# Cross attention and a 4-bit dense layer on one core: the softmax weights are turned by VectorE in squares of 32 and regrouped through DRAM, instead of by TensorE transposes

## What is computed

```
q = layernorm(x) @ Wq        # 32 heads of 128
k = ctx @ Wk; v = ctx @ Wv   # 8 heads of 128, each shared by 4 query heads
q, k = rope(q, pos), rope(k, pos)
scores = q k^T / sqrt(128), set to -1e9 where mask == 0
attn = softmax(scores);  x = x + concat(attn v) @ Wo
x = x + layernorm(x) @ dequantize(qweight, qzeros, scales) + bias
```

## Time and profile before

| | |
|---|---|
| median of 3 runs | 2412.4 us (2410.72 to 2417.8) |
| the profiled execution's own time | 2418.64 us |
| its span, first to last instruction | 2416.8 us, granted clock 0.991 |
| PE busy | 2353.0 us, 97% |
| DVE, ACT, POOL busy | 1336.1, 1114.9, 1180.8 us (55%, 46%, 49%) |
| stage B (first `score` to last `out_copy`) | about 405 to 1596 us |
| mean DMA rate | 143 GB/s |

### The profile page before, as it was taken

How to read it: one execution, slowest core, us unless ns; L and a number is a source line. 1 busy time by engine, 2 the same in 40 slices (tenths; PEclk the granted TensorE clock), 3 DMA queues, 4 the chain that set the end, 5 groups by cost and what they waited for, 6 DMA issues and landing times.

```text
span 2416.8 us, 33647 instructions
## 1 busy us (share of the span) xinstructions
PE 2353.0 (97%) x11552; PEld 1975.2 (82%) x11552; DVE 1336.1 (55%) x1949; ACT 1114.9 (46%) x2515; POOL 1180.8 (49%) x926
## 2 busy tenths in 40 slices
PE   8999998999999999899999999989999999999999
PEld 6887877888888888688888888868887877878887
DVE  4762554666666666666666666637743233343532
ACT  3222123667676667666766667643332222322010
POOL 1410535555665665556665566555664344355110
PEclk9999999999999999999999999999999999999999
DMA  7676674333434335343343333368554454443111
GB/s 262 237 178 223 233 246 152 92 102 100 113 103 114 105 106 155 113 127 102 93 117 106 106 112 103 111 212 284 202 191 168 149 178 166 143 177 113 44 44 53
DMA packets 201241, 346.65 MB, mean 143 GB/s; under 512 B 17744, under 2 KB 126544, under 8 KB 201168
## 3 DMA queue, kind: packets, MB, share of 16 engines
q1 hardware_dynamic: 187088, 310.06, 41.0%
q10 hardware_dynamic: 13312, 33.56, 4.2%
q0 software_dynamic: 768, 2.10, 0.3%
HBM read 238.69 MB, written 106.97 MB: 143 GB/s over the span
## 4 chain that ended last, share of the span: by engine, by line
PE 81%; DVE 7%; DMA 5%; ACT 3%; POOL 3%; issue 1%; SPq 1%; ACTq 0%; DVEq 0%; POOLq 0%
PE ps L208 18%; PE ps L209 18%; PE ps L210 18%; PE ps L690 7%; PE ps L691 7%; PE ps L692 7%; PE ps L622 4%; DMA scores<-in_ctx 2%; DVE rows L1226 1%; DMA xc_scratch<-xring 1%; DMA wraw<-in_L_xattn_Wo 1%; DMA xring<-in_x_tiles 1%; POOL s_buf L1322 1%; ACT probs L864 1%; PE ps L714 1%
## 5 line engine op out<-in xcount | busy, mean ns | idle before, releaser
L208 PE MATMUL ps<-act_t,wq_t 128*128 128x512 f32 x1280 | 512.5, 400 | 20.8 <-DVE act_t L1076 10.9
L210 PE MATMUL ps<-act_t,wq_t 128*128 128x512 f32 x1280 | 501.8, 392 | 0.0
L209 PE MATMUL ps<-act_t,wq_t 128*128 128x512 f32 x1280 | 501.6, 392 | 0.0
L690 PE MATMUL ps<-b_parts,a_parts 128*128 128x512 f32 x896 | 353.1, 394 | 11.3 <-POOL b_parts L1395 5.1
L1322 POOL TENSOR_TENSOR rope_tmp<-rope_tmp 128x512 f32<-128x512 f32 x144 | 192.4, 1336 | 341.8 <-DVE rope_tmp L1013 341.7
L691 PE MATMUL ps<-b_parts,a_parts 128*128 128x512 f32 x896 | 350.1, 391 | 0.0
L692 PE MATMUL ps<-b_parts,a_parts 128*128 128x512 f32 x896 | 349.7, 390 | 0.0
L1171 DVE TENSOR_TENSOR a_parts<-xring,a_parts 128x1024 fp32r<-128x1024 f32 x112 | 147.8, 1320 | 349.7 <-ACT a_parts L889 349.7
L1395 POOL TENSOR_TENSOR b_parts<-wraw,b_parts 128x512 fp32r<-128x512 f32 x112 | 195.7, 1748 | 275.1 <-ACT b_parts L894 275.1
L889 ACT ACTIVATE a_parts<-xring 128x1024 fp32r<-128x1024 f32 x112 | 118.7, 1060 | 415.8 <-PE ps L692 407.8
L208 PEld LDWEIGHTS ps<-act_t,wq_t 128*128 128x128 f32 x1280 | 242.5, 189 | 69.7 <-DVE act_t L1076 11.4
(11 more groups left out here) (111 smaller groups left out, 4437.8 us busy)
## 6 DMA issues: line engine op xcount, KB each, us to landing
xring<-left_scratch SPq DMA_DIRECT2D x112, 512.0 KB, 3.5
left_scratch<-s_buf SPq DMA_DIRECT2D x64, 640.0 KB, 5.3
wraw<-in_L_xattn_Wq SPq DMA_DIRECT2D x64, 512.0 KB, 4.0
wraw<-in_L_xattn_Wo SPq DMA_DIRECT2D x64, 512.0 KB, 4.4
v_scratch<-kv_t ACTq DMA_DIRECT2D x32, 512.0 KB, 3.0
k_scratch<-kv_t ACTq DMA_DIRECT2D x32, 512.0 KB, 5.1
kv_t<-k_scratch SPq DMA_DIRECT2D x64, 256.0 KB, 5.1
kv_t<-v_scratch SPq DMA_DIRECT2D x64, 256.0 KB, 4.6
```

The lines of the kernel that those rows point to most:

```text
L208: eng.matmul(dst, lh, rh, start=(k == first), stop=False)
L209: eng.matmul(dst, lh, rl, start=False, stop=False)
L210: mm = eng.matmul(dst, ll, rh, start=False, stop=(k == last))
L690: pe.matmul(dst, lh, rh, start=(begins and not onto), stop=False, skip_group_check=True)
```

## The change

The eight `turn` transposes of a unit leave PE, except in the last four units (`tail`). In their place:

- DVE `transpose_squares` turns the weights in squares of 32x32 (one instruction of 128x1024) into `squares`; SP `store_squares` writes them to DRAM (512 KB), and when that has landed, SP `load_turned` reads them back with four DMAs, each of which fills 32 partitions (128 KB, in runs of 1 KB), which puts every square on its partitions; ACT `turned_hi` and POOL `turned_lo` (128x1024 each) make the two parts.
- `weigh` comes two units after its unit instead of one. The banks of scores and outputs are doubled, which the two banks of the transposes make room for.
- `masked` is now one instruction for each 128x256 that adds a mask (0 or -1e30) and takes the minimum of the negated sum (`tensor_tensor_reduce`, followed by a read of the accumulator); `exponents` uses scale -1.
- `out_copy` moves from ACT to DVE, `head_lo` from POOL to DVE (`next_head_lo`, behind `inverse_sum`). POOL's `combine` is spread over two units.
- The splitting of the second half's activations moves from group 7 to group 0: for each of eight pieces SP `load_centred`, ACT `split_piece`, DVE `rest_of_piece`, and two ACT-issued stores `store_parts`. Group 7 then loads high and low parts straight into `act_t` (sixteen DMAs of 512 KB, eight before unit 2 and eight before unit 4).

The core of the diff:

```
-            def weigh(G, u8, first=False):
+            def weigh(G, u8, fresh=False, tail=False):
...
-                    pe.wait_ge(o_copied, G * UPG + u8)
+                    pe.wait_ge(o_copied, G * UPG + (u8 - 1))
...
+                    pe.wait_ge(pt_lo, G * UPG + (u8 + 1))
...
+            def transpose_squares(G, u8):
+                par = u8 % 2
+                dve.wait_ge(p_ready, G * UPG + (u8 + 1))
+                dve.transpose(squares[par].rearrange("p (b k n i) -> p k n b i", b=4, k=2, n=4),
+                              probs[:, par, :, :, :].rearrange("p j q (k b i) -> p k (j q) b i", k=2, b=4)
+                              ).then_inc(squared, 1)
...
+            def store_squares(G, u8):
+                sp.wait_ge(squared, G * UPG + (u8 + 1))
+                sp.dma_start(sq_dram[u8 % 4], squares[u8 % 2].rearrange("p (b n) -> p b n", b=4)
+                             ).then_inc(sq_stored[u8 % 2], 16)
+
+            def load_turned(G, u8, first=False):
+
+                sp.wait_ge(sq_stored[u8 % 2], G * 64 + (u8 // 2 * 16 + 16))
+                if not first:
+                    hold(sp)
+                    sp.wait_ge(pt_lo, G * UPG + (u8 - 1))
+                for b in range(4):
+                    sp.dma_start(pt_raw[32 * b:32 * b + 32, u8 % 2, :].rearrange("i (a n) -> i a n", a=4),
+                                 sq_dram[u8 % 4, :, b, :].rearrange("(a i) n -> i a n", a=4)).then_inc(pt_in[u8 % 2], 16)
...
+            def turned_hi(G, u8, first=False):
+                act.wait_ge(pt_in[u8 % 2], G * 256 + (u8 // 2 * 64 + 64))
+                if not first:
+                    act.wait_ge(av_done, G * UPG + (u8 - 1))
+                act.activation(probs_t[u8 % 2][:, 0, :, :, :].rearrange("p a k n -> p (a k n)"), pt_raw[:, u8 % 2, :],
+                               ACT.Copy).then_inc(pt_hi, 1)
...
+            def turned_lo(G, u8):
+                pool.wait_ge(pt_hi, G * UPG + (u8 + 1))
+                hi, lo = [probs_t[u8 % 2][:, l, :, :, :].rearrange("p a k n -> p (a k n)") for l in range(2)]
+                pool.tensor_tensor(lo, pt_raw[:, u8 % 2, :], hi.bitcast(F32), ALU.subtract).then_inc(pt_lo, 1)
...
+            def load_centred(i):
+
+                if i > 0:
+                    sp.wait_ge(parts_stored, i * 32)
+                sp.dma_start(x_pair[0], xc_dram[i]).then_inc(xc_in, 16)
...
+            def split_piece(i):
+                act.wait_ge(xc_in, (i + 1) * 16)
+                act.activation(x_pair[1].bitcast(F32R), x_pair[0], ACT.Copy).then_inc(piece_hi, 1)
+
+            def store_parts(i):
+                act.wait_ge(piece_lo, i + 1)
+                act.dma_start(xp_dram[i, 0], x_pair[1]).then_inc(parts_stored, 16)
+                act.dma_start(xp_dram[i, 1], x_pair[0]).then_inc(parts_stored, 16)
...
+            def rest_of_piece(i):
+                dve.wait_ge(piece_hi, i + 1)
+                dve.tensor_tensor(x_pair[0].bitcast(F32R), x_pair[0], x_pair[1], ALU.subtract).then_inc(piece_lo, 1)
```

More of the change, by code:

```diff
@@ L406, in attention @@
                     p = (G - half * 8) * 2 + par
+                    tail = last and par == 1
                     if switch and u8 in (2, 4):
@@ L437, in attention @@
                             sp.dma_start(rope[:, c, :, :], rope_dram[1, c]).then_inc(rope_in[c], 16)
-                if not last:
-                    sp.wait_ge(av_done, G * UPG + UPG)
-                    load_v(g, HB - 1, nh)
-                else:
+                    if first and u8 > 0:
+                        load_centred(u8)
+                if last:
                     load_step(2)
                     load_step(3)
-                store_group(G * 4 + 3, half, (G - half * 8) * 2 + 1, 1, 1)
+                    for q in (62, 63):
+                        store_outputs(q, 31, q % 2)
+                        store_sums(q, 31, q % 2)
             def load_step(s):
@@ L628, in attention @@
                     i, pair = u8 % 4, G * 2 + (u8 // 4 + 1)
-                    more = not (last and u8 >= 4)
                     if u8 < UPG - 1:
-                        score(G, u8 + 1)
+                        score(G, u8 + 1, fresh=first and u8 == 0)
                     elif not last:
                         score(G + 1, 0)
-                    if u8 > 0:
-                        weigh(G, u8 - 1, first=first and u8 == 1)
+                    if last and u8 >= 4:
+                        if u8 < 6:
+                            weigh(G, u8 - 2)
+                        if u8 > 4:
+                            weigh(G, u8 - 1, tail=True)
+                        turn(u8)
+                        continue
@@ L636, in attention @@
+                    if switch and u8 in (4, 6):
+                        for k in range(2):
+                            pe.wait_ge(xp_in[2 * (u8 - 4) + k], 32)
+                    query(pair, i, 0, G * UPG + (u8 + 4))
+                    if u8 >= 2:
+                        weigh(G, u8 - 2, fresh=first and u8 < 4)
                     elif not first:
-                        weigh(G - 1, UPG - 1)
+                        weigh(G - 1, UPG + u8 - 2)
                     if switch and u8 in (4, 6):
-                        pe.wait_ge(x_lo, TT + 2 * (u8 - 4) + 2)
@@ L641, in attention @@
-                    if more:
-                        query(pair, i, 0, G * UPG + (u8 + 4))
-                    turn(G, u8, first=first and u8 == 0)
-                    if switch and u8 in (4, 6):
-                        pe.wait_ge(x_lo, TT + 2 * (u8 - 4) + 4)
-                    if more:
-                        query(pair, i, 1, G * UPG + (u8 + 4))
+                        for k in range(2, 4):
+                            pe.wait_ge(xp_in[2 * (u8 - 4) + k], 32)
+                    query(pair, i, 1, G * UPG + (u8 + 4))
@@ L661, in _ @@
             pe.wait_ge(kv_lo, UNITS_A)
[L662 removed]
+            score(0, 0, first=True, fresh=True)
             attention(0, first=True)
@@ L934, in attention @@
                         scaled(nG, nxt)
-            for m in range(3):
-                query_hi(0, 0, m, m)
+                    if first:
+                        split_piece(u8)
+            act.wait_ge(ident_in, 16)
+            act.activation(row_sum[:, 0, 0, 0:1], identity[:, 0:1], ACT.Exp)
+            query_hi(FIRST_TILES[0], 0)
+            head_hi(0, 10 * 16, (q_done, 2))
+            query_hi(FIRST_TILES[1], 1)
+            query_hi(FIRST_TILES[2], 2)
             exponents(0, 0)
-            head_hi(0, 10 * 16, (q_done, 3))
             scaled(0, 0)
@@ L1448, in _ @@
             attention(15, last=True)
-            combine(63, 1, (left_stored[0], 32 * 48))
+            for q in (62, 63):
+                for part in range(2):
+                    combine(q, q % 2, part)
             right_summed(2)
```

415 lines of the change are left out of this document (239 added, 176 removed).

## The result

| | before | after |
|---|---|---|
| median | 2413.01 us (2410.72 to 2417.8, 4 runs) | 2440.34 us (2434.39 to 2441.88, 4 runs) |
| profiled execution | 2418.64 us | 2434.39 us |
| its span, granted clock | 2416.8 us, 0.991 | 2432.6 us, 0.981 |

The ratio of the medians is 1.0105 (95% interval 1.0092 to 1.0117). The forecast was 2363 us, so its direction was wrong. The time lies inside the range for 8 in 10 (2325 to 2450), near its upper end, and outside the forecast's own 2340 to 2395. Both profiled executions lie some 6 us from their medians, on opposite sides: the traces show 15.8 us of loss where the medians show 27.3.

A forecast was written before the change was run, and what follows sets the result against it. PE, busy 97% of the span, was taken as the bound. From 2418.6 us, -108 + 17 + 45 - 7 + 0 + 4 = -49 gave 2369.6; the median, 6.2 lower, 2363 us, own range 2340 to 2395, 8 in 10 from 2325 to 2450.

The forecast's parts named there:

- What leaves PE: Attention units: 124 of 128 lose eight transposes, 0.87 us each, together 108 us; a unit falls from 9.14 to 8.27.
- The other engines' sums: Per attention unit: POOL 6.9 us, ACT 5.9, DVE 6.8 (bounds 6.1 to 8.4), to fit into 8.27.
- Hidden, then, with a thin margin: DRAM round trip of 7.7 us lands at T'+3.0, harmless until T'+3.1; T' is the next unit's score start.
- The first rival: Loops: the DRAM round trip becomes the bound, setting the pace from a trip of 9.0 us; slower; 2 in 10.
- ACT waiting for `pt_raw`: In the profile after: this wait in every unit would show that the round trip had become the bound.
- A wait of 0.5 us, once in four units: Loops: PE's `query` waits for `next_head_lo` on DVE, itself held by POOL's `turned_lo`; 17 us in all.
- Group 0: Piece loop of 14.7 us replaces 8.27 for seven rounds, +45 us; PE's 7.3 us idle start lies inside, -7.
- Group 7 at 0: Squares late by 7 to 9 us, 3 to 4 of it slack, twice; equals the old loss: 0, bounds -8 and +16.
- The queue's own sum: Loops: bytes per two units rise from 1920 to 3968 KB, DMA share from 38% to about 87%, an upper estimate.
- The end: After the attention: POOL has two whole `combine` ahead of the sums for step 2, before one; +4 us.
- The chances: Whole kernel: faster by over 0.3% 0.66, same 0.08, slower 0.26.
- the third rival: Group 0 doesn't loop as written, because transfers land faster and the pieces hide: 2325 us; 1 in 10.

The follow-up runs named there:

- Experiment 12: Changed kernel with the head's split early on DVE, sums issued by ACT, no pieces in group 0, group 7 loading 4 MB and splitting in place: 2334.88 us.
- 6: Changed kernel with the head's split on DVE directly behind `masked` and the 640 KB of sums issued by ACT: 2404.79 us, ratio 0.9949.
- experiment 3: Changed kernel whose four loads read other DRAM data without waiting for the squares' store to land: 2426.01 us, ratio 1.0059.
- 5: Changed kernel with the 640 KB of sums issued by ACT in odd units, not by SP ahead of the loads: 2441.18 us, ratio 1.0105.
- 2: Changed kernel with the next head's split on DVE directly behind `masked`, ahead of the output's copy and reciprocal: 2432.35 us, ratio 1.0093.
- experiment 4: Changed kernel without the eight pieces in group 0; group 7 loads the unsplit data twice: 2395.93 us, ratio 0.9934.
- 9: Changed kernel with group 7's sixteen loads issued in four lots of four, not two of eight: 2447.87 us, ratio 1.0135.
- 11: Changed kernel without group 7's sixteen loads and PE's waits for them: 2422.12 us, ratio 1.003.
- 10: Changed kernel with the head's split early on DVE, sums issued by ACT, and no pieces in group 0, group 7 loading unsplit data: 2340.77 us, ratio 0.9695.
- 7: Changed kernel with the pieces spread over groups 0 and 1, one in two units: 2431.2 us, ratio 1.0061.

## Why the prediction was wrong

**What leaves PE: right.** Experiment 12 has units of 67.2 / 8 = 8.40 us in the loops, where the forecast's were 8.41 and PE alone would need 8.27; the undisturbed units of the changed kernel start 8.26 apart.

**The other engines' sums: right, where they were disputed.** The transpose took 1.245 (1.22 taken, 1.07 by the other estimate), `turned_lo` 2.62 on average (2.41), `turned_hi` 1.06 (1.05). `masked` came out smaller: 0.411 and 0.083, but the pairs start 0.34 apart, four in about 1.4 us and not 2.06. No engine became the bound.

**"Hidden, then, with a thin margin": the step that failed.** The trip took 9.2 us, not 7.7, and the squares were ready 0.4 later. In odd units the mis-sized term is the four loads: 6.3 us from the first issue to the last landing, not 4.7, with the 640 KB of sums ahead of them; the load's issue came as forecast (2.9 us after the store's, 3.0 taken). In even units it is the store: it landed in 4.4 us and not 3.0. The turned weights came at T'+4.9, past the T'+3.1 that the forecast itself named as the last harmless moment, and `query_hi` and the exponents behind them came 2 us later than forecast (their end at T'+8.8, not T'+6.8). The forecast priced the 128 KB by rows of a quieter queue (1.8 us; 3.1 after), though it had itself worked out that the load on the queue would double. Its lower bound of 5.9 for the trip isn't what its terms give either: 2.6 + 1.9 + 1.8 is 6.3.

The first rival had its threshold at a trip of 9.0, but its mechanism, a pace set by the trip alone, isn't what happened: it would slow every unit, and five of eight ran at 8.3 to 8.5. Its sign, ACT waiting for `pt_raw`, came true here and just as much in experiment 12, where it costs almost nothing, so it was no sign. And with trips as long (9.6 and 9.5 us in odd units) the loops ran at 67.8 (6) and 67.2 (12). The length of the trip did harm only through what stood behind it. Whether a trip of 7.7 us would have been enough by itself wasn't tested: neither experiment 3 nor 5 shortened it in odd units.

**"A wait of 0.5 us, once in four units": mis-sized by the same lateness.** The mechanism is in the rows as foretold (2.71 behind POOL, PE released by `wq_t`), but the late exponents move the split later: PE waited 1.5 us for it on average and up to 1.7 in the loops, once in four units. Experiments 2, 5 and 6 show that the split's place and the late query tile each cover the other. Both together are the loops' 47 us of the miss: with both edits a group took 67.8 us (6) or 67.2 (12), and the forecast's was 67.3.

**Group 0: the loop was right, the 7 us taken off were not.** The first two of ACT's splits are 14.78 us apart, and the eight 15.2 on average, where 14.7 was worked out:

```profile
412.06 1.04 ACT L881 ACTIVATE xring<-xring 128x1024 fp32r<-128x1024 f32 x1
...
426.84 1.06 ACT L881 ACTIVATE xring<-xring 128x1024 fp32r<-128x1024 f32 x1 [4.40 <-DMA xring<-xc_scratch]
```

Seven rounds of 15.2 are 48 us more than seven units of 8.27; +45 was forecast. But the net cost by experiment 4 is 38.8 us in the group and 10.7 ahead of its first copy, 49.5 and not 45 - 7: the idle time of PE at the start wasn't swallowed by the rounds, the first of which lies ahead of the first copy.

**Group 7 at 0: wrong by 9 us.** The squares' store stands behind eight loads, 4 MB. It was issued at 971.27, and the loads of the squares followed at 982.89:

```profile
982.89 1.75 SPq L426 DMA_DIRECT2D pt_raw<-sq_scratch  x4
...
987.33 1.06 ACT L970 ACTIVATE q_t<-pt_raw 128x1024 fp32r<-128x1024 f32 x1 [12.20 <-DMA pt_raw<-sq_scratch]
...
994.22 0.76 PE L227 MATMUL ps<-act_t,wq_t 128*128 128x512 f32 x1 [12.60 <-DVE wq_t L1301]
```

This trip took 16.1 us, 7 more than in the loops, as was forecast (7 to 9). But the slack of 3 to 4 us wasn't there, since the trips of the loops were late already, and behind it came the exponents, the reciprocal and then the head's split. PE waited 12.6 us for that split; for the activations themselves it never waited. What makes the trip long is the bytes rather than their order. Between 985 and 1005 us the DMA engines were busy 0.99 of the time at 332 GB/s, PE waited, and its granted clock averaged 0.66 (1.00 is the level of 2.4 GHz, 0.5 that of 1.2) behind idle time of PE that had begun in the window before. Smaller lots changed nothing (9), no loads made it 74.1 (11), and half the bytes, with the splits back in the group, 85.7 where the same kernel with all of them had 92.6 (12 against 10). The queue's own sum was in the forecast (87% in the loops; 75% was measured), but not applied to the place with 8 MB more. The Trainium skill (DMA: Bandwidth & Descriptors, section "Where 436 GB/s comes from") gives 435 GB/s for the ports of SBUF and about 358 for a core's share of the HBM (the DRAM of this text), and says that the latter binds for transfers between the two. The trace agrees: at a share of 0.99 this mix of transfers moved 332, a little below.

**The end: right.** +5.2 us against +4.

**The chances:** 0.66 for faster doesn't agree with the parts, of which the forecast (0.6) and the third rival (0.1) alone make 0.7.

**The balance** of the traces: 47 (loops) + 9 (group 7) + 8 - 3 (start and group 15) + 4 (group 0) + 1 (end) = 66, and the spans differ by 2432.6 - 2367.8 = 65. The 12 of start and group 0 are 11.5 for the pieces beyond the forecast, 3.5 for the loops' loss in group 0 too (70.8 without pieces, not 67.3) and 2 for the later `weigh`, less the 5 of the shorter stage A. Another 12 us lie between the two profiled executions and their medians. The scatter of stage A (7 us between the traces) can be a part of it; no row explains the rest.

**What stays open:** whether a shorter trip alone would have saved the loops, what exactly costs 3.1 us a piece when it has two units to itself (7), and the 4 us more of group 7 with both edits while the pieces are there (6).

## What to carry to other kernels

When a step is moved from a saturated engine to a DMA round trip, walk each DMA through its queue in every variant of the loop body, with landing times for the load that the change itself creates, and look at what stands behind its landing: the trip was as long in the fastest kernel as in the slow one. When two waits end close together, removing either shows almost nothing: test them in pairs before calling one harmless. And moving work off a place where PE waits anyway can cost more than it saved, both where it arrives and in the bytes that it leaves behind.

## What was not expected of the hardware

- The landing time of a 128 KB DMA to or from DRAM doubled with the traffic around it, 1.8 to 3.7 us for the same store, while the DMA engines were busy only 0.75 of the time (0.38 before).
- A `tensor_tensor_reduce` of 128x256 out of PSUM overlaps the next: 411 ns and an accumulator read of 83 ns, and yet one pair every 0.34 us.
- The head's split on DVE, alone 1.22 us by the earlier trace rows, took 2.09 on average, and its mean tells nothing of its cost: what counts is whether POOL has begun before it.
